# A gated mixture kernel: the second mixture's routing weights spread over partitions by transfers from DRAM, and half of the weighing moved to GpSimd

## The reference

```python
logits = x @ gate_w.T                       # 64 experts
w = softmax(logits), kept for the top 8, divided by their sum, 0 for the others
y = sum over experts e of w[e] * (silu(x @ w_gate[e].T) * (x @ w_up[e].T)) @ w_down[e].T
x = x + tanh(g) * y
```

## Time and profile before

| | |
|---|---|
| median of 3 runs | 809.14 us (805.01 to 813.88) |
| the profiled execution | 814.23 us, of which the span of the trace is 812.4 us |
| second mixture in the trace, first silu to the copy of its sum | 446.65 to 657.06 us |
| busy over the span | PE 657.7, DVE 613.8, ACT 361.5, POOL 332.7 us |

### The profile page before, as it was taken

One profiled execution on the slowest core, in us unless ns is written; L12 is line 12 of the kernel. 1 busy time (PEld: TensorE's weight loads), 2 busy tenths in 40 slices (PEclk: granted clock), 3 DMA queues, 4 the chain that ended last, 5 costly groups with the idle time before them and its releaser, 6 DMA issues.

```text
span 812.4 us, 16859 instructions
## 1 busy us (share of the span) xinstructions
PE 657.7 (81%) x5096; PEld 311.1 (38%) x5096; DVE 613.8 (76%) x1169; ACT 361.5 (44%) x629; POOL 332.7 (41%) x570
## 2 busy tenths in 40 slices
PE   1259926999986884879972999999999967996796
PEld 0023313444433662335541444444444433554342
DVE  5558773677767776747965899999999976575696
ACT  1314412999935440613231454554555544333453
POOL 4066613677710272126662354454444410125151
PEclk9755555999968796869985999999999997998799
DMA  8000000111131000000000121121111100000010
GB/s 272 0 0 1 0 0 14 43 49 48 44 83 44 2 3 1 0 1 2 2 2 10 47 57 51 51 55 53 50 55 55 55 5 1 2 2 9 26 57 27
DMA packets 41784, 26.05 MB, mean 32 GB/s; under 512 B 12664, under 2 KB 40616, under 8 KB 41569
## 3 DMA queue, kind: packets, MB, share of 16 engines
q1 hardware_dynamic: 40184, 23.31, 10.2%
q10 hardware_dynamic: 1552, 2.11, 0.8%
HBM read 24.85 MB, written 0.56 MB: 31 GB/s over the span
## 4 chain that ended last, share of the span: by engine, by line
PE 66%; DVE 19%; issue 6%; POOL 4%; ACT 2%; DMA 2%; SPq 1%; POOLq 0%; DVEq 0%; ACTq 0%
PE PS L190 52%; PE PS L453 4%; DVE SHARED L977 2%; DVE MB L1011 2%; PE PS L1099 2%; PE PS L990 2%; DMA BF<-in_brow 2%; PE PS L1105 2%; DVE MF L1011 1%; DVE REC L1113 1%; PE PS L1064 1%; DVE XN L309 1%; DVE STAT L293 1%; POOL RSTD L327 1%; DVE SHARED L746 1%
## 5 line engine op out<-in xcount | busy, mean ns | idle before, releaser
L755 DVE TENSOR_TENSOR SHARED<-SHARED 128x512 f16<-128x512 f32 x180 | 142.1, 796 | 36.3 <-ACT SHARED L737 35.4
L737 ACT ACTIVATE SHARED<-SHARED 128x512 f16<-128x512 f32 x180 | 113.4, 630 | 121.5 <-DVE SHARED L749 115.0
L190 PE MATMUL PS<-XH,UH 128*128 128x512 f16 x296 | 114.8, 388 | 2.2 <-ACT CT L560 2.2
L190 PE MATMUL PS<-XL,UH 128*128 128x512 f16 x296 | 114.7, 388 | 0.0
L190 PE MATMUL PS<-XH,UL 128*128 128x512 f16 x296 | 114.5, 387 | 0.0
L190 PE MATMUL PS<-SHARED,DNH 128*128 128x512 f16 x360 | 107.1, 379 | 5.3 <-DVE SHARED L755 5.2
L1082 ACT ACTIVATE SHARED<-PS 128x512 f32<-128x512 f32 x96 | 52.5, 595 | 100.4 <-PE PS L190 75.3
L746 DVE TENSOR_TENSOR SHARED<-SHARED,PS 128x512 f32<-128x512 f32 x116 | 78.6, 678 | 12.5 <-PE PS L190 12.5
L668 POOL CAST DNH<-DF 128x128 f16<-128x128 f32 x90 | 31.5, 350 | 129.5 <-PE PS L190 129.5
L749 DVE TENSOR_TENSOR SHARED<-SHARED,PS 128x512 f32<-128x512 f32 x116 | 79.7, 687 | 4.0
L658 POOL TENSOR_TENSOR UL<-UF,UH 128x256 f16<-128x256 f32 (+1 forms) x90 | 69.5, 772 | 7.2
(11 more groups left out here) (267 smaller groups left out, 1231.2 us busy)
## 6 DMA issues: line engine op xcount, KB each, us to landing
UF<-in_up SPq DMA_DIRECT2D x58, 128.0 KB, 2.0
DF<-in_down SPq DMA_DIRECT2D x90, 64.0 KB, 1.8
UF<-in_up SPq DMA_DIRECT2D x32, 64.0 KB, 1.8
SHARED<-t_values_dram SPq DMA_DIRECT2D x2, 1024.0 KB, 10.7
SEL<-in_sel SPq DMA_DIRECT2D x58, 32.0 KB, 1.7
SHARED<-in_masks ACTq DMA_DIRECT2D x1, 1024.0 KB, 9.1
WF<-in_wsmall SPq DMA_DIRECT2D x1, 868.0 KB, 5.5
X<-in_x SPq DMA_DIRECT2D x1, 512.0 KB, 3.7
```

Of the source, the lines that this page charges most:

```text
L190: last = pe.matmul(dst, l, r, start=start and i == 0, stop=stop and i == len(pairs) - 1)
L737: act.activation(HHI[:, u, hf, :], (HF if M["gated"] else RH[u])[:, hf, :], ACT.Copy).then_inc(sem("e_high"), 1)
L755: dve.tensor_tensor(HLO[:, u, hf, :], src[:, hf, :], HHI[:, u, hf, :], ALU.subtract).then_inc(sem("e_low"), 1)
```

## The change

- `route_pe`, m=1: the logits go to bank 6 in place of bank 2, and the turning of `CW` is gone. `route_dve` stops after L593; `route_act` after the exponential. The products of chunk 0 no longer wait for the routing.
- `LE` is turned in fp32 by 8 PE transposes (banks 4 and 5), copied by two ACT instructions to `WROWS` (64 experts x 1024 tokens) and written by SP to a DRAM tensor `w1`. SP then loads, for each chunk, the 4 KB row of each of its two experts into all the partitions that belong to it: two transfers with a repeated source row, together 128 x 4 KB, into `WB[c % 2]`. This takes the place of the `SEL` load of m=1.
- The two selector matmuls of each chunk are gone.
- Half 0: POOL computes `TG = SG * WB` (128 x 512, fp32), then DVE computes `HF = TG * bank(2)`. Half 1: DVE computes `TG = SG * bank(3)` and `HF = TG * WB`. The low parts stay on DVE, the high parts on ACT, in the order that they had.
- POOL's order in a chunk is: the multiplication for half 0, the split of `UF` of chunk c+2, the split of `DF` of chunk c+1.
- m=2 keeps its selector products; its counters no longer start behind those of m=1, and POOL's split of `UF` waits for the up products where it waited for the selector products.

```diff
@@ route_pe / route_dve
+            if m == 1:
+                logits = bank(6)[:, 0:NB * E].rearrange("p (b e) -> p b e", b=NB)
...
+            if m == 1:
+                return
+            pe.wait_ge(sem("r_weights"), m // 2 + 1)
...
-                step(dve.tensor_tensor(le, le, along(ZS[:, 3, :], E), ALU.mult))
-                step(dve.tensor_copy(CW[:, :, 0:E], le))
-                dve.tensor_tensor(CW[:, :, E:2 * E], le, CW[:, :, 0:E], ALU.subtract).then_inc(sem("r_weights"), 1)
+                dve.tensor_tensor(le, le, along(ZS[:, 3, :], E), ALU.mult).then_inc(sem("w1_weights"), 1)
@@ moe_pe_up
             if M["gated"]:
-                if not (isinstance(ga, int) and ga == 0):
+                if m == 1 and not (isinstance(c, int) and c == 0):
+                    if hf == 0:
+                        pe.wait_ge(sem("w1_first"), c)
+                    else:
+                        pe.wait_ge(sem("w1_gated"), c)
+                if m == 2 and not (isinstance(ga, int) and ga == 0):
                     pe.wait_ge(sem("e_gated"), 2 * ga + hf - 1)
                 products(pe, bank(2 + hf), three(UH[:, u, 128:256], UL[:, u, 128:256], XHh[hf], XLh[hf]))\
-                    .then_inc(sem("e_up"), 1)
-            if not M["gated"]:
+                    .then_inc(sem(f"e_up{m}"), 1)
+            if m < 2:
                 return
@@ moe_act_silu
+                    elif hf == 0:
+                        act.wait_ge(sem("w1_weighed"), c)
+                    else:
+                        act.wait_ge(sem("w1_gated"), c)
                 act.activation(SG[:, hf, :], bank(hf), ACT.Silu).then_inc(sem("e_act"), 1)
@@ moe_act_high
-            if M["gated"]:
-                act.wait_ge(sem("e_hidden"), 2 * (M["gat"] + c) + hf + 1)
+            if m == 1:
+                act.wait_ge(sem("w1_second" if hf else "w1_first"), c + 1)
@@ new
+        def moe1_pool_weigh(pool, c, u, h):
+            pool.wait_ge(sem("e_act"), 2 * (CH0 + c) + 1)
+            pool.wait_ge(sem(f"w1_in{u}"), 32 * h + 32)
+            if not (isinstance(c, int) and c == 0):
+                pool.wait_ge(sem("w1_first"), c)
+            pool.tensor_tensor(TG[:, 0, :], SG[:, 0, :], WB[u][:, 0:HALF], ALU.mult).then_inc(sem("w1_weighed"), 1)
+        def moe1_dve_first(dve, c):
+            dve.wait_ge(sem("w1_weighed"), c + 1)
+            dve.wait_ge(sem("e_up1"), 2 * c + 1)
+            dve.wait_ge(sem("e_low"), 2 * (CH0 + c) - 1)
+            dve.tensor_tensor(HF[:, 0, :], TG[:, 0, :], bank(2), ALU.mult).then_inc(sem("w1_first"), 1)
+        def moe1_dve_second(dve, c, u, h):
+            dve.wait_ge(sem("e_act"), 2 * (CH0 + c) + 2)
+            dve.wait_ge(sem("e_up1"), 2 * c + 2)
+            if not (isinstance(c, int) and c == 0):
+                dve.wait_ge(sem("w1_second"), c)
+            dve.tensor_tensor(TG[:, 1, :], SG[:, 1, :], bank(3), ALU.mult).then_inc(sem("w1_gated"), 1)
+            dve.wait_ge(sem("w1_gated"), c + 1)
+            dve.wait_ge(sem(f"w1_in{u}"), 32 * h + 32)
+            dve.wait_ge(sem("e_low"), 2 * (CH0 + c))
+            dve.tensor_tensor(HF[:, 1, :], TG[:, 1, :], WB[u][:, HALF:TOK], ALU.mult).then_inc(sem("w1_second"), 1)
+        SPANS = (((0, 96, 0), (96, 128, 1)), ((0, 64, 1), (64, 128, 2)), ((0, 32, 2), (32, 128, 3)))
+        def moe1_sp_weights(sp, c, ex, k):
+            if not (isinstance(c, int) and c < 2):
+                sp.wait_ge(sem("w1_first"), c - 1)
+                sp.wait_ge(sem("w1_second"), c - 1)
+            for lo, hi, j in SPANS[k % 3]:
+                settled(sp, "sp")
+                sp.dma_start(WB[k % 2][lo:hi, :], t["w1"][bass.ds(ex + j, 1), :].to_broadcast([hi - lo, TOK]))                    .then_inc(sem(f"w1_in{k % 2}"), 16)
+        def moe1_sp(sp):
...
+            sp.wait_ge(sem("w1_rows"), 2)
+            sp.dma_start(t["w1"], WROWS).then_inc(sem("w1_out"), 16)
+            sp.wait_ge(sem("w1_out"), 16)
+            def step(c, ex, k, up=True, down=True):
+                moe1_sp_weights(sp, c, ex, k)
+                if up:
+                    moe1_sp_up(sp, c + 2, k % 2)
+                if down:
+                    moe1_sp_down(sp, c + 1, 1 - k % 2)
@@ moe_pe, step
                 for hf in range(2):
                     moe_pe_up(pe, m, c, u, h, hf)
+                if m == 1 and isinstance(c, int) and c == 0:
+                    moe1_rows_pe(pe)
@@ moe_act, step
                 for hf in range(2):
                     moe_act_silu(act, m, c, u, hf)
+                if m == 1 and isinstance(c, int) and c == 0:
+                    moe1_rows_act(act)
                 for hf in range(2):
                     moe_act_high(act, m, c, u, hf)
@@ moe_dve, step
+                if m == 1:
+                    moe1_dve_first(dve, c)
+                    moe1_dve_second(dve, c, u, h)
```

More of the change, by code:

```diff
@@ L177, in gated_mix_program @@
         OWN = piece(3072, 1024).rearrange("p (i n) -> p i n", i=2)
+        WB = [piece(at, 1024) for at in (8192, 9216)]
+        WROWS = piece(10240, 1024, parts=E2)
         PKI, PKE = sb("PKI", [128, 32], i32), sb("PKE", [128, 4, 32], i32)
@@ new lines, in moe1_sp_weights @@
+        def moe1_sp_weights(sp, c, ex, k):
+            if not (isinstance(c, int) and c < 2):
+                sp.wait_ge(sem("w1_first"), c - 1)
+                sp.wait_ge(sem("w1_second"), c - 1)
+            for lo, hi, j in SPANS[k % 3]:
+                settled(sp, "sp")
+                sp.dma_start(WB[k % 2][lo:hi, :], t["w1"][bass.ds(ex + j, 1), :].to_broadcast([hi - lo, TOK]))                    .then_inc(sem(f"w1_in{k % 2}"), 16)
+        def moe1_sp(sp):
+            moe1_sp_up(sp, 0, 0)
+            moe1_sp_up(sp, 1, 1)
+            moe1_sp_down(sp, 0, 0)
+            sp.wait_ge(sem("w1_rows"), 2)
[7 more added lines that the diff above has]
+                    moe1_sp_down(sp, c + 1, 1 - k % 2)
+            for k in range(6):
+                step(k, 4 * (k // 3), k)
+            with sp.Fori(1, CH2 // 6 - 1) as i:
+                for k in range(6):
+                    step(6 * i + k, 8 * i + 4 * (k // 3), k)
+            for k in range(6):
+                c = CH2 - 6 + k
+                step(c, 4 * (c // 3), k, up=k < 4, down=k < 5)
@@ new lines, in moe1_pool, with step @@
+        def moe1_pool(pool):
+            moe_pool_up(pool, 1, 0, 0, 0)
+            moe_pool_up(pool, 1, 1, 1, 0)
+            moe_pool_down(pool, 1, 0, 0, 0)
+            def step(c, u, h, up=True, down=True):
+                moe1_pool_weigh(pool, c, u, h)
+                if up:
+                    moe_pool_up(pool, 1, c + 2, u, h + 1)
+                if down:
+                    moe_pool_down(pool, 1, c + 1, 1 - u, h + u)
+            step(0, 0, 0)
+            step(1, 1, 0)
+            with pool.Fori(1, CH2 // 2 - 1) as i:
+                step(2 * i, 0, i)
+                step(2 * i + 1, 1, i)
+            step(CH2 - 2, 0, CH2 // 2 - 1, up=False)
+            step(CH2 - 1, 1, CH2 // 2 - 1, up=False, down=False)
@@ new lines, in moe1_rows_pe, with moe1_rows_act @@
+        def moe1_rows_pe(pe):
+            pe.wait_ge(sem("w1_weights"), 1)
+            for b in range(NB):
+                last = pe.transpose(bank(4 + b // 4)[0:E2, 128 * (b % 4):128 * (b % 4) + 128], LE[:, b, :], EYE[:])
+                if b % 4 == 3:
+                    last.then_inc(sem("w1_turned"), 1)
+        def moe1_rows_act(act):
+            for i in range(2):
+                act.wait_ge(sem("w1_turned"), i + 1)
+                act.activation(WROWS[:, HALF * i:HALF * i + HALF], bank(4 + i)[0:E2, :], ACT.Copy).then_inc(sem("w1_rows"), 1)
@@ L842, in moe_loads @@
         def moe_loads(sp, m):
+            if m == 1:
+                moe1_sp(sp)
+                return
             chunks(sp, m, lambda c, u, h: moe_sp(sp, m, c, u, first=m == 0 and isinstance(c, int)))
         def moe_pool(pool, m):
+            if m == 1:
+                moe1_pool(pool)
+                return
             def step(c, u, h):
@@ L895, in step @@
             def step(c, u, h):
-                for hf in range(2):
-                    moe_dve_hidden(dve, m, c, u, hf)
+                if m == 1:
+                    moe1_dve_first(dve, c)
+                    moe1_dve_second(dve, c, u, h)
+                else:
+                    for hf in range(2):
+                        moe_dve_hidden(dve, m, c, u, hf)
                 for hf in range(2):
```

47 lines of the change are left out of this document (28 added, 19 removed).

## The result

The changed kernel takes 847.6 us (median of 4 runs, 844.6 to 848.7), the kernel before, timed beside it, 810.1 us (4 runs): a difference of 37.5 us and a ratio of 1.0461, 95% interval 1.0396 to 1.0526. The prediction had 24.2 us more. The span of the profiled execution went from 812.4 to 845.9 us.

A forecast was written before the change was run, and what follows sets the result against it. PE's matmuls and an ACT-DVE handover chain were taken as equal bounds. 449.2 + 47 x 4.80 = 674.8 against 651.06, with the tail +24.2 us on 809.1, gave 833 us; range 817 to 852.

The forecast's parts named there:

- the rival in which the ports add 0.4 us: Second mixture's loop: blocking at ports shared by DVE and GpSimd lengthens the chain to 5.2 us, 852 us in all; 15%.
- Two bounds at the same height before the change: Second mixture's loop: PE's matmuls, 4.28 us a chunk, and a closing chain of ACT and DVE handovers, 4.31 us.
- The chain closes on itself through ACT's order, with GpSimd in it: Changed loop: next silu 0 stands behind high 1, which waits through DVE for GpSimd and silu 0; 4.74 us before ports.
- the signs: Loop profile: PE below 85%, silu 0 every 4.8 us, no ACT gap before it, DVE idle about 1 us for GpSimd.
- The sentence on what is added to the old chain and what is gone: Loop chain: adds GpSimd in series (1.27 + 0.25); removes one DVE product (0.60) and the low part (0.91 - 0.08).
- Its length, 4.80: Loop chain per chunk: steps sum to 4.74 us, plus 0.06 for ports, with 4.55 and 5.2 as ends.
- The wakings: Loop handovers: GpSimd starts 0.15 us after silu 0 (0.10 to 0.25), DVE 0.10 after GpSimd (0.03 to 0.20).
- The ports: Loop: GpSimd and two-input DVE instructions block each other at shared SBUF ports; 0.06 us a chunk (0 to 0.4).
- The transfers: Loop: the `WB` load takes 4.0 us with issue, a buffer loop of 3.8 us a chunk, hidden with 2.0 us spare.
- The head, +2.6 us: Before the loop: turning, writing and loading weights moves the start of the pace from 446.65 to 449.2.
- The tail, +0.45 us: End of the second mixture: from the last silu 0 to the copy, 6.45 us against 6.00.
- The prediction's break-even: Whole kernel: no gain or loss at a chain of 4.28 us, GpSimd's product at 0.75; landing within 1%: 4%.

The follow-up runs named there:

- opening ACT's order: The changed kernel with GpSimd's product given back to DVE and ACT's silu 0 of the next chunk ahead of high 1: 817.9 us, pace 4.35.
- the order alone: The changed kernel with ACT running high 0, next chunk's silu 0, high 1, next chunk's silu 1: 827.5 us, pace 4.58.
- the run with the late wait last: The changed kernel with the waits of three instructions reordered, so that the late one comes last: 847.7 us, pace 4.99.
- without the splits: The changed kernel with GpSimd's four weight splits cut to 16 columns from chunk 2 on: 847.3 us, pace 5.04.
- the versions that opened the chain and kept GpSimd's product: The changed kernel with silu 0 ahead of high 1, alone or with late waits last, short splits, or short splits and loads: 827.5, 828.4, 823.3, 820.9 us.
- the half-width run: The changed kernel with GpSimd weighing 256 of the 512 columns of half 0: ratio 1.022 against the kernel before, pace 4.56.
- on DVE, waits included: DVE weighs both halves, silu 0 ahead, late waits last, half 1's low part behind the next chunk's first product: 807.4 us against 808.5 before.
- the version with silu 0 ahead and splits of 16 columns: The changed kernel with next chunk's silu 0 ahead of high 1 and GpSimd's four splits at 16 columns from chunk 2: 823.3 us, pace 4.48.

## Why the prediction was right, and what it undersized

The time fell into the range (817 to 852), and the cause is the forecast one: GpSimd's product in series in a chain that closes through ACT. The size was not met: 37.5 us came for 24.2, and the pace of 5.10 lies above the 4.55 to 5.0 that the forecast gave itself. The range held because its top was set for the rival in which the ports add 0.4 us; what in fact filled that room was longer handovers. That part is luck. By its steps:

- *Two bounds at the same height before the change.* Borne out in height, not in kind. With 18 matmuls and GpSimd out of it the pace stayed at 4.37. But opening ACT's order then changed nothing (4.35), so the second bound of that version is DVE's six instructions with their gaps, not the circle through silu 0. That version weighs with `WB` in SBUF where the kernel before reads PSUM, and the kernel before with only its selector matmuls taken away was not run.
- *The chain closes on itself through ACT's order, with GpSimd in it.* Shown three ways: the order alone is worth 0.52 us a chunk, half of GpSimd's product 0.54 for 0.54, all of it 0.73. Of the signs, silu 0 starts every 5.10 us for 4.8, ACT has no gap before it, and DVE waits 1.5 us for GpSimd where about 1 was said; PE's 86% busy misses "below 85%" by a point. The sentence on what is added to the old chain and what is gone makes 0.09 us of the 0.43 between 4.31 and 4.74; it leaves out mainly that silu 0 and high 1 now both stand in the chain. The sum itself is right.
- *Its length, 4.80: the term that was undersized.* It measured 5.10; the 0.3 us makes 14 of the 16.7 us by which the stretch of the mixture outran the forecast (40.9 against 24.2). The durations were right: silu 0.58, GpSimd 1.26 for 1.27, 0.60 between independent products. The wakings were not: to GpSimd 0.16 and 0.24 in turn for 0.15, to DVE 0.25 for 0.10. Together they make 0.20 of the 0.3. They were read at rows with 0.10 and 0.03 and got 0.05 and 0.07 us more for the three waits of the new instructions; the run with the late wait last shows that the order of those waits alone is worth 0.09 and 0.21. The product with `WB`: 0.90 to its start and 0.69 long, or 0.71 and 0.81, together 1.55 for the 1.47 (0.72, 0.69, 0.06) forecast.
- *The ports.* Right as a mechanism and, at 0.06 us a chunk, right in size (5.10 to 5.04 without the splits). The rival in which they decide, 5.2 us, did not come true in this kernel. In the versions that opened the chain and kept GpSimd's product (4.45 to 4.58) the stretched instructions point to them.
- *The transfers.* Hidden, as forecast: a load of 384 KB landed in 3.7 us, and from chunk 1 on both loads of a chunk were in 1.1 to 2.6 us before GpSimd's product began.
- *The head, +2.6 us.* GpSimd's first product started 11.2 us after the last routing product began (444.84 - 433.64), where 8.9 was forecast: turning and copying came 0.5 us later than forecast (the eight fp32 transposes took 1.91 us, the fp16 ones 1.03, both at a granted clock of about 0.5), the write to DRAM took 3.1 for 2.2, the first load 4.8 for 3.9. Up to silu 0 of chunk 2 the forecast makes +3.5 (2.6 and two turns of 0.45), and +4.6 was measured.
- *The tail, +0.45 us.* 1.7 measured. The last six matmuls started 0.43 us apart where 0.21 is the distance at the full clock, which makes the missing 1.3 us: PE had been idle for 3.17 us before them, and the granted clock of 685 to 690 us was 0.68 (a mean of the two levels). In the kernel before, the same six came after 2.19 us of waiting and ran at 1.00.
- *The clock in the loop.* 1.00 at 86% busy, as forecast.

The prediction's break-even, GpSimd's product at 0.75 us or less, can be held against the half-width run: at 0.725 the kernel was still 17 us above the one before. The break-even rested on the same wakings, head and tail, each taken too small.

## What to carry to other kernels

Before work is moved to an idle engine, write down the handovers of one turn of the loop in the order in which each engine runs them, and add up the circle that closes; an engine that is half idle, as GpSimd was in the loop, adds its whole instruction to that circle if its result is waited for at once. Here two bounds stood at about the same height, so relieving PE gained nothing while DVE's order stayed as it was, and changing the order on ACT (20 us) and on DVE, waits included (10 us), was worth more than the 96 matmuls. In a long chain it can help to put the wait that comes last at the end of an instruction's list of waits; here it gave 0.11 us a chunk and no time that the runs could tell, because the earlier start collided with GpSimd.

## What the runs showed of the hardware

- The order of an instruction's waits has a price, but no fixed one: with the late wait last in place of first of three, the handover from GpSimd to DVE went from 0.25 to 0.03 us, the one from ACT to GpSimd from a mean of 0.20 to 0.11, and the one between two dependent DVE products from 0.80 to 0.81.
- The blocking between GpSimd and DVE includes GpSimd's casts with one input: the 128 x 256 cast went from 0.40 to a mean of 0.78, and in the version with silu 0 ahead and splits of 16 columns the first cast and the last subtraction, 0.20 and 0.22 us in the changed kernel at that width, had means of 0.57 and 0.59.
- Loads whose 128 partitions read the same one or two DRAM rows landed in 3.1 to 4.0 us (medians for 128 to 384 KB, with 144 GB/s of traffic in all). The 128 KB loads of `UF`, each partition from its own row, took 3.5 in the same trace, so no sign of a slow shared row was seen.
